# B's transposes moved between u and the first mix, its copies split over two engines, and four loads regrouped, in a fused adaptive-norm FFN kernel

## The reference

```
# layer 0
att   = softmax(mlp(cond))                            # (128, 8)
agg_w = einsum('bk,koi->boi', att, weight)            # a 32x32 mix for each sample
y     = einsum('boi,bih->boh', agg_w, x) + (att @ bias_k)[:, :, None]
gates = softmax(top2(y @ Wr.T))                       # 4 experts
x     = x + sum_e gates[e] * (y @ A[e].T) @ B[e].T * 4
# layer 1
o     = conv1d(x, convw, groups=4, 9 taps) + cond @ ctx_w.T + bias
w     = top-2 softmax weights of 8 experts, from relu(layernorm(o @ gw1.T + gb1)) @ gw2.T,
        zeroed for experts over a capacity that is counted over all tokens
x     = x + o @ weight.T + sum_e w[e] * (o @ lora_A[e]) @ lora_B[e] / 16
```

## Time and profile before

| | us |
|---|---|
| median of 3 runs | 302.68 |
| the three runs | 301.27, 302.68, 303.99 |
| the profiled execution | 302.07 |
| its span, first to last instruction | 300.3 |
| PE busy in it | 288.7 |

### The profile page before, as it was taken

One profiled execution on the slowest core, in us unless ns is written; L12 is line 12 of the kernel. 1 busy time (PEld: TensorE's weight loads), 2 busy tenths in 40 slices (PEclk: granted clock), 3 DMA queues, 4 the chain that ended last, 5 costly groups with the idle time before them and its releaser, 6 DMA issues.

```text
span 300.3 us, 6135 instructions
## 1 busy us (share of the span) xinstructions
PE 288.7 (96%) x1982; PEld 236.5 (79%) x1982; DVE 195.4 (65%) x506; ACT 125.3 (42%) x263; POOL 95.1 (32%) x124
## 2 busy tenths in 40 slices
PE   7999979999999999999999999999999999999994
PEld 5788957687978797879877987798777876777883
DVE  1655964743669466946594749474948555899885
ACT  3325834434622572258224822392237326103430
POOL 4361425123311431143114311431113235217660
PEclk9999999999999999999999999999999999999998
DMA  5796699893869487946794669458646790005887
GB/s 142 186 339 143 154 252 233 212 213 75 220 185 210 87 218 211 178 93 181 228 189 104 161 224 207 104 154 204 129 104 163 187 206 6 0 2 188 320 331 280
DMA packets 74400, 52.75 MB, mean 176 GB/s; under 512 B 44405, under 2 KB 61477, under 8 KB 74377
## 3 DMA queue, kind: packets, MB, share of 16 engines
q1 hardware_dynamic: 72936, 51.37, 69.1%
q10 hardware_dynamic: 1120, 1.07, 1.1%
q0 software_dynamic: 320, 0.02, 0.2%
HBM read 35.67 MB, written 16.78 MB: 175 GB/s over the span
## 4 chain that ended last, share of the span: by engine, by line
PE 54%; DMA 14%; SPq 12%; DVE 8%; issue 5%; ACT 4%; POOL 1%; DVEq 0%; ACTq 0%
PE ps_g L1139 10%; PE ps_d L1139 9%; DMA xg<-x1d 8%; PE ps_c L1277 7%; DMA x1d<-xq 7%; PE ps_a L1100 5%; PE ps_t L1293 3%; SPq L353 3%; PE ps_a L1089 3%; SPq L356 2%; ACT xq L632 2%; PE ps_d L1318 2%; PE ps_d L1319 2%; PE ps_d L1500 1%; PE ps_d L1505 1%
## 5 line engine op out<-in xcount | busy, mean ns | idle before, releaser
L512 POOL TENSOR_TENSOR o1l<-o,o1h 128x512 fp32r<-128x512 f32 x30 | 39.4, 1313 | 150.2 <-ACT o L644 150.2
L1139 PE MATMUL ps_d<-wt_hi,o1h 128*128 128x336 f32 (+1 forms) x120 | 41.1, 342 | 0.3 <-DVE y_all L961 0.3
L1139 PE MATMUL ps_d<-wt_hi,o1l 128*128 128x336 f32 (+1 forms) x120 | 38.7, 323 | 0.0
L1139 PE MATMUL ps_d<-wt_lo,o1h 128*128 128x336 f32 (+1 forms) x120 | 38.6, 322 | 0.0
L1277 PE MATMUL ps_c<-xg,cw 96*32 96x512 f32 x256 | 34.1, 604 | 3.1 <-DMA xg<-x1d 3.1
L955 DVE TENSOR_TENSOR oT<-ps_c,biasT 128x512 f32<-128x512 f32 x32 | 21.9, 686 | 22.8 <-PE ps_c L1277 21.9
L1139 PE MATMUL ps_g<-wt_hi,o1h 128*128 128x336 f32 x112 | 35.6, 318 | 0.6 <-ACT tmp_all L659 0.4
L1139 PE MATMUL ps_g<-wt_hi,o1l 128*128 128x336 f32 x112 | 35.5, 317 | 0.0
L1139 PE MATMUL ps_g<-wt_lo,o1h 128*128 128x336 f32 x112 | 35.4, 316 | 0.0
L632 ACT ACTIVATE xq<-y_all 128x512 f32 (+1 forms) x29 | 31.9, 1152 | 7.3 <-DMA x1d<-xq 4.1
L1100 PEld LDWEIGHTS ps_a<-pm,xT 128*128 128x128 f32 x256 | 30.2, 192 | 1.4 <-issue 0.8
(11 more groups left out here) (258 smaller groups left out, 577.7 us busy)
## 6 DMA issues: line engine op xcount, KB each, us to landing
xg<-x1d SPq DMA_DIRECT2D x64, 254.0 KB, 5.1
xg<-x1d SPq DMA_DIRECT2D x32, 256.0 KB, 3.8
x1d<-xq SPq DMA_DIRECT2D x30, 256.0 KB, 3.6
xs<-in_x_dram SPq DMA_DIRECT2D x6, 1024.0 KB, 6.2
out_dram<-xT SPq DMA_DIRECT2D x16, 256.0 KB, 2.1
out_dram<-xg SPq DMA_DIRECT2D x15, 256.0 KB, 2.1
y_all<-in_x_dram ACTq DMA_DIRECT2D x2, 512.0 KB, 5.2
y_all<-in_x_dram SPq DMA_DIRECT2D x1, 1024.0 KB, 5.7
```

The lines of the kernel that those rows point to most:

```text
L512: pool.tensor_tensor(lo, o1[t % 2][:, :, :], hi.bitcast(fp32), ALU.subtract).then_inc(s_o1l, 1)
L1139: last = T.matmul(bank[:, 0:columns], a[:, Q - 1 - q, :], w[:, q, first:first + columns], start=(q == 0 and n == 0), stop=(q == Q - 1 and ...
```

## The change

B's four transposes on PE move from between the first two tiles of `u_products(0)` to behind the last of them, where a fill stood. ScalarE copies the result twice, plain (`b_plain`, new) and rounded to `b_hi`; VectorE subtracts the two into `b_lo` behind `gates0(0)`, where before it made both parts from PSUM ahead of `mixbd`. `delta(0, 0)` waits for it. The transposes of `aw` move ahead of `attT`'s and VectorE's copy of them ahead of the context's; a second fill goes. The `aw` loads go ahead of the `mixw` loads. `bex`'s transpose and its copy to `biasT` move behind the first two transposes of step 1.

`ga` gets another layout, in blocks of 16 columns, so that one load with runs of 256 bytes brings all of `lora_a`, where eight with runs of 64 bytes did, and it is issued ahead of the taps. The x load of step 3 leaves the setup and is issued in SP's step 1, where the later steps have theirs.

```diff
@@ -29,6 +29,7 @@
...
     GC = G1 + ER1
+    GB = G1 // R1
     MC = (H + GC) // 2
@@ -63,6 +64,9 @@
...
             return v.broadcast_to(shape)
+
+        def blocks(v):
+            return v.rearrange("p q (e r) -> p e q r", r=R1)
@@ -92,7 +96,7 @@
...
         b_lo = sb("b_lo", [P, H], fp32r)
-        ga = sb("ga", [P, Q, GC])
+        ga = sb("ga", [P, GC // R1, Q, R1])
         cw = sb("cw", [P, G, Q, CG])
@@ -175,6 +179,7 @@
...
         pmsum = early(P, [UC])
+        b_plain = early(P, [HC, P])
@@ -200,7 +205,7 @@
...
         s_wk0 = sem("mix_zeros_ready")
-        names = ("condT", "pm", "h1", "ctxT", "b", "h2", "gw1", "att", "ctx", "rs", "attT", "wkr", "bias", "pmsum")
+        names = ("condT", "pm", "h1", "ctxT", "b", "h2", "gw1", "att", "ctx", "rs", "attT", "wkr", "bias", "pmsum", "b_hi", "b_plain")
         s_sp = {n: sem(f"setup_ps_{n}") for n in names}
@@ -331,13 +336,13 @@
...
             sp.dma_start(w2n, w2).then_inc(s_ld["w2"], 16)
+            sp.dma_start(aw[0:ER0], ffa.rearrange("e r h -> (e r) h")).then_inc(s_ld["aw"], 16)
+            sp.dma_start(aw[ER0:UC], ffr).then_inc(s_ld["aw"], 16)
             sp.wait_ge(s_wk0, 1)
...
                   .then_inc(s_ld["mixw"], 16)
-            sp.dma_start(aw[0:ER0], ffa.rearrange("e r h -> (e r) h")).then_inc(s_ld["aw"], 16)
-            sp.dma_start(aw[ER0:UC], ffr).then_inc(s_ld["aw"], 16)
             sp.dma_start(mbn, row(mixb, 1, BT)).then_inc(s_ld["mixb"], 16)
@@ -346,15 +351,13 @@
...
             sp.dma_start(gw2n, row(gw2, 1, NT)).then_inc(s_ld["gate"], 16)
-            for i in range(2):
-                sp.dma_start(xs[i][:, :, :], x_v[2 + i]).then_inc(s_x[i], 16)
+            sp.dma_start(xs[0][:, :, :], x_v[2]).then_inc(s_x[0], 16)
+            sp.dma_start(ga[:, GB:, :, :].rearrange("p e q r -> p e (q r)"),
+                         lora_a.rearrange("e (m q) r -> m e (q r)", q=Q)).then_inc(s_ld["lora_a"], 16)
             sp.wait_ge(s_zero, 1)
...
                              convw.rearrange("o c k -> c o k")).then_inc(s_ld["conv"], 16)
-            for e in range(E1):
-                sp.dma_start(ga[:, :, G1 + e * R1:G1 + (e + 1) * R1],
-                             lora_a[e].rearrange("(m q) r -> m q r", q=Q)).then_inc(s_ld["lora_a"], 16)
@@ -401,7 +404,7 @@
...
                         wait(sp, s_x1w[2], (s + 1) * 32)
-                if has(s, 2) and not at_step(s, 0) and not at_step(s, 1):
+                if has(s, 2) and not at_step(s, 0):
@@ -520,8 +523,8 @@
...
                     pool.wait_ge(s_gm, 2)
-                    pool.tensor_tensor(wt_lo[:, :, H:H + GC], ga[:, :, :], wt_hi[:, :, H:H + GC].bitcast(fp32),
-                                       ALU.subtract).then_inc(s_gal, 1)
+                    pool.tensor_tensor(blocks(wt_lo[:, :, H:H + GC]), ga[:, :, :, :],
+                                       blocks(wt_hi[:, :, H:H + GC].bitcast(fp32)), ALU.subtract).then_inc(s_gal, 1)
                     o1_low(0, 0)
@@ -599,8 +602,10 @@
...
             u_out(0)
-            act.wait_ge(s_sp["bias"], 1)
-            nc.scalar.activation(biasT[:, :], ps_t[:, 0:NB], ACT.Copy).then_inc(s_ss["bias"], 1)
+            act.wait_ge(s_sp["b"], 1)
+            nc.scalar.activation(b_plain.rearrange("p c m -> p (c m)"), ps_t[:, :], ACT.Copy).then_inc(s_ss["b_plain"], 1)
+            nc.scalar.activation(b_hi[:, :].rearrange("p (m c) -> p c m", c=HC),
+                                 ps_t[:, :].rearrange("p (c m) -> p c m", c=HC), ACT.Copy).then_inc(s_ss["b_hi"], 1)
@@ -608,6 +613,8 @@
...
             x_transposed(1, (0, 1))
+            act.wait_ge(s_sp["bias"], 1)
+            nc.scalar.activation(biasT[:, :], ps_t[:, 0:NB], ACT.Copy).then_inc(s_ss["bias"], 1)
             mix_copied(1, 2)
@@ -705,8 +712,8 @@
...
                     act.wait_ge(s_ss["gw1"], 1)
-                    act.wait_ge(s_ld["lora_a"], 16 * E1)
-                    nc.scalar.activation(wt_hi[:, :, H:H + GC], ga[:, :, :], ACT.Copy).then_inc(s_gah, 1)
+                    act.wait_ge(s_ld["lora_a"], 16)
+                    nc.scalar.activation(blocks(wt_hi[:, :, H:H + GC]), ga[:, :, :, :], ACT.Copy).then_inc(s_gah, 1)
                     gm_out(1)
@@ -833,6 +840,8 @@
...
             V.tensor_scalar(attw[:, :, 0:K0], row(atte, 1, 4), sm[:, 2:3], None, ALU.mult).then_inc(s_ss["att"], 1)
+            dve.wait_ge(s_sp["pm"], 1)
+            V.tensor_copy(pm[:, :, :].rearrange("p c u -> p (c u)"), ps_t[:, 0:HC * UC]).then_inc(s_ss["pm"], 1)
             dve.wait_ge(s_sp["ctx"], 1)
@@ -842,17 +851,9 @@
...
             V.tensor_copy(attT, ps_v[:, 0:P]).then_inc(s_ss["attT"], 1)
-            dve.wait_ge(s_sp["pm"], 1)
-            V.tensor_copy(pm[:, :, :].rearrange("p c u -> p (c u)"), ps_t[:, 0:HC * UC]).then_inc(s_ss["pm"], 1)
             dve.wait_ge(s_ss["pm"], 1)
...
-            dve.wait_ge(s_sp["b"], 1)
-            b_in = ps_t[:, :].rearrange("p (c m) -> p c m", c=HC)
-            link(V.tensor_copy(b_hi[:, :].rearrange("p (m c) -> p c m", c=HC), b_in))
-            V.tensor_tensor(b_lo[:, :].rearrange("p (m c) -> p c m", c=HC), b_in,
-                            b_hi[:, :].bitcast(fp32).rearrange("p (m c) -> p c m", c=HC),
-                            ALU.subtract).then_inc(s_ss["b"], 1)
             dve.wait_ge(s_mp0, 1)
@@ -863,6 +864,11 @@
...
             gates0(0)
+            dve.wait_ge(s_ss["b_hi"], 1)
+            dve.wait_ge(s_ss["b_plain"], 1)
+            V.tensor_tensor(b_lo[:, :].rearrange("p (m c) -> p c m", c=HC), b_plain,
+                            b_hi[:, :].bitcast(fp32).rearrange("p (m c) -> p c m", c=HC),
+                            ALU.subtract).then_inc(s_ss["b"], 1)
             dve.wait_ge(s_ld["rows"], 16 * 2)
@@ -970,7 +976,7 @@
...
                                       ps_v[G1 * t:G1 * t + G1, Q * G1:Q * G1 + E1])
-                    V.tensor_copy(ga[:, :, 0:G1], ps_v[:, 0:Q * G1].rearrange("p (q g) -> p q g", q=Q))\
+                    V.tensor_copy(ga[:, 0:GB, :, :], ps_v[:, 0:Q * G1].rearrange("p (q e r) -> p e q r", q=Q, r=R1))\
                      .then_inc(s_ss["gw1"], 1)
@@ -1186,25 +1192,20 @@
...
             t1(0, xs_early[0], 1)
-            keep_busy(1)
+            pe.wait_ge(s_ld["aw"], 32)
+            pe.wait_ge(s_attd, 1)
+            for c in range(HC):
+                last = T.transpose(ps_t[:, c * UC:(c + 1) * UC], aw[:, c * P:(c + 1) * P], ident[0:UC, 0:UC])
+            last.then_inc(s_sp["pm"], 1)
             pe.wait_ge(s_ss["att"], 1)
...
             t1(0, xs_early[0], 2)
-            pe.wait_ge(s_ld["aw"], 32)
-            for c in range(HC):
-                last = T.transpose(ps_t[:, c * UC:(c + 1) * UC], aw[:, c * P:(c + 1) * P], ident[0:UC, 0:UC])
-            last.then_inc(s_sp["pm"], 1)
             pe.wait_ge(s_xt, 2)
...
             pe.wait_ge(s_ss["pm"], 1)
-            u_products(0, (0,))
-            pe.wait_ge(s_bn, 1)
-            for c in range(HC):
-                last = T.transpose(ps_t[:, c * P:(c + 1) * P], bn2[:, c, :, :].rearrange("p d e -> p (d e)"), idp)
-            last.then_inc(s_sp["b"], 1)
-            u_products(0, (1,))
+            u_products(0, (0, 1))
             pe.wait_ge(s_attD, 1)
@@ -1218,13 +1219,14 @@
...
             u_products(0, (2, 3))
+            pe.wait_ge(s_bn, 1)
+            for c in range(HC):
+                last = T.transpose(ps_t[:, c * P:(c + 1) * P], bn2[:, c, :, :].rearrange("p d e -> p (d e)"), idp)
+            last.then_inc(s_sp["b"], 1)
             pe.wait_ge(s_bd, 1)
-            keep_busy(1)
             pe.wait_ge(s_mbsb, 1)
...
             mix(0)
-            pe.wait_ge(s_ss["b"], 1)
-            T.transpose(ps_t[:, 0:NB], bex, idp).then_inc(s_sp["bias"], 1)
@@ -1240,6 +1242,9 @@
...
             pe.wait_ge(s_ss["ctx"], 1)
+            pe.wait_ge(s_ss["b_hi"], 1)
+            pe.wait_ge(s_ss["b_plain"], 1)
+            T.transpose(ps_t[:, 0:NB], bex, idp).then_inc(s_sp["bias"], 1)
             mixture(1)
@@ -1304,7 +1309,7 @@
...
                         last = T.matmul(ps_g[:, 0:GC], o1[t % 2][:, Q - 1 - q, :],
-                                        ga[:, q, :], start=(q == 0), stop=(q == Q - 1))
+                                        ga[:, :, q, :], start=(q == 0), stop=(q == Q - 1))
                     last.then_inc(s_gp, 1)
@@ -1360,6 +1365,7 @@
...
                     pe.wait_ge(s_msa, 4)
+                    pe.wait_ge(s_ss["b"], 1)
                     delta(0, 0)
...
```

## The result

| | median, us | range | executions |
|---|---|---|---|
| before | 303.34 | 301.27 to 305.29 | 4 |
| the change | 307.62 | 304.87 to 308.39 | 4 |

The ratio is 1.019, 95% interval [1.013, 1.025]: some 2% slower, where 301.4 us and "about the same" were forecast. The profiled execution took 308.39 us, its span is 306.7, against 302.07 and 300.3. Such a ratio can mislead: the kernel before, timed once more against itself, came out at 1.0145 [1.0065, 1.0225] (experiment 4). What follows therefore rests on rows of the traces more than on this ratio.

The account below looks back on a forecast made before the run. TensorE, busy 288.7 of 300.3 us, bounds the kernel. -3.37 at conv(1,0) and +2.05 for the moved load give -1.3: span 299.0, 300.8 profiled, 301.4 on the median; range 299.2 to 303.5.

Parts of the forecast that it names:

- The load that is moved: SP's step 1: x3 ahead of gather(1,1) adds 2.8 us; PE stands 2.0, conv(1,1) starts at 63.05, gain 1.3.
- The price: x3's megabyte, added whole to gather(1,1)'s landing: 2.8 us taken, 2.4 by the landings' spacing, upper bound 4.2.
- The landing without x3: gather(1,1)'s landing before x3's price is added: 64.05 less 3.85 us, from an earlier gather(1,0).
- 378 GB/s: Mean DMA rate over the 2 us in which step 2 takes its x load; it priced 1.05 MB at 2.8 us.
- the 3.5: Upper sign before conv(1,1): the prediction is wrong if the idle there is under 1 or over 3.5 us.
- Rival 3: Clock falls in the setup or at the stand before conv(1,1); 4 us of matmuls at half speed give 305.4; chance 0.06.
- The setup: PE's work up to mix(0): earlier `aw` and moved transposes start mix(0) at 17.7 instead of 19.11, -1.4 us.
- nothing gained: Bound on `aw`'s landing in the setup: still 10.16, where 7.1 was taken from its 3.1 us earlier issue.
- SP's release: SP's queue free between 17 and 26.8 us, hidden because the first x1 tile is reordered only at 27.4.
- the gain at conv(0,0): No idle before conv(0,0), which starts near 36.6 us: -3.3.
- B's parts: ScalarE's copies (0.6 and 0.9 us) and VectorE's b_lo behind gates0(0) are free, 0.2 us to spare before delta(0,0).
- The rule: Transposes don't count as PE activity for the clock gate, so fewer fills and a 2 us stand would be riskier.

Follow-up runs that it names:

- experiment 4: Kernel before: one `lora_a` load 300.42 us; unchanged 305.38; four fills before conv(0,0) 301.68. The change with x3's load in the setup and eight `lora_a` loads: 304.94.
- experiment 3: Against the change: gather(1,2) issued only after gather(1,1) has landed, 307.03 us; x3's load issued behind gather(1,1) instead of ahead, 302.32 us.
- behind the taps: The change with x3's load back in the setup, issued behind the taps' loads: 301.21 us.
- the setup's order alone: The change with x3's load back in the setup and `lora_a` in eight loads behind the taps with the old `ga` layout: 304.94 us.
- the half behind: The change with x3's load in the setup and the second half of step 0's x on SP's queue behind `aw`: 299.57 us, ratio 0.995.

## Why the prediction was wrong

**The step that failed** is "The load that is moved": "I add the megabyte whole ... I take 2.8", "PE stands 2.0 us there". gather(1,1) landed at 67.06 in the profile (65.86 in the second), not at 63.0: the price of x3's load was taken too small, and the landing to which it was added too early.

*The price.* With x3 ahead, the gather's last part took 9.4 to 10.3 us from issue to landing (9.2 with (1,2) held back); without, 5.8 to 6.1 in four profiles. That is 3.3 to 4.5, and with the 0.5 that x3's own issue holds SP 3.8 to 5.0, where 2.8 were taken and 4.2 was the upper bound. 3.4 of it is the load's by experiment 3. That gather(1,2) takes part in the rest is possible, not shown; the prediction let it only "catch up".

*The landing without x3.* The step implies 60.2. Without x3 ahead of it the gather landed at 61.0 (behind the taps), 61.1 (x3 behind the gather) and 62.5 (in the setup). In the terms of the step, its last part was issued 2.66 later than implied (56.76 for 57.95 - 3.85 = 54.10), and from issue to landing went 10.30 instead of 6.1 + 2.8 = 8.9, so 1.40 more; together 4.06. Of the 2.66 some 2.0 stood before x3 was issued: gather(1,0) went at 51.73, not 3.85 ahead of its old 53.57.

*What the trace of before had.* The 378 GB/s are no price of the load by itself: in that trace the engines moved nearly as much from 58 to 60 us, when no x load was in flight. And its step 2 has the very order that the change makes in step 1, x's load right ahead of gather(2,1). SP in order of time, that part's source view, and the window:

```profile
86.53 0.86 SPq L376 DMA_DIRECT2D xg<-x1d  x1
```

```profile
DMA to landing us min/median/max: 8.1/8.1/8.1
```

```profile
58.00:60.00 2.00, 1.58 (x13) 0.54 (x11) 1.79 (x7) 0.00 (x0) 0.35 (x1) 1.00 1.08 355
```

8.1 us behind the load, with the engines all but empty (under 13 GB/s from 84 to 86) when it was issued; in the change they moved 216 to 290 when x3 was issued, and it took 10.3. The price had to be asked of the gather behind the load, and of what was in flight already. The stand, 3.6 to 4.8, passed the 3.5 that the prediction named as the point at which it would be wrong.

**The clock** was held up by the 1.97 us that "left the clock up" in one profile. That was one draw of two outcomes: the kernel before loses its clock in about four executions of ten (39 of 92), in the one that was profiled behind 2.23 us of idle. Rival 3 (slower, 305.4, given 0.06) named the mechanism and one of its places, and was priced too low by the stand: of the 6.4 us lost in the profile 2.9 are the clock's, the rest is waiting, net of the early gain. From 67 to 73 us the clock stood at 0.50, six us in which about three us' worth of work was done. The prediction read a single execution's clock row as a property of the kernel.

**The setup**: -1.4 at mix(0) was -0.19. `aw`, issued at 3.1, landed at 10.1 as before; "nothing gained" was named as a bound, and was true. Behind it sat a second step that the prediction passed over: the transposes of x's third and fourth tile are now queued behind `pm`'s on PE, so the xT copies that u_products waits for came at 11.16 instead of 10.01 + 0.60. With `aw` on time the gain was 0.5, so even the better landing is not worth 1.4. Whether the MLP's chain, 0.6 to 0.8 us later (ScalarE's exponential at 8.97 and 8.82 in the change's two profiles and 9.06 with the half behind, for 8.21), is also the loads' doing was not tried.

**Right were**: SP's release by 25.7 (within 17 to 26.8) and its being hidden, the first write as soon as its tile was there (28.70; forecast 27.5, late by the setup's 1.2), no idle before conv(0,0), 0.30 before gm_transposed(1) (forecast 0.35), the gain at conv(0,0) but for the setup's share (37.74; 36.6) and so at conv(0,1) (43.08; 41.9) and conv(1,0) (56.99; 55.71). B's parts were free: ScalarE, and VectorE's low part behind the gates, in order of time:

```profile
18.70 0.60 ACT L606 ACTIVATE y_all<-ps_t 128x512 f32<-128x512 f32 x1
19.20 1.09 ACT L607 ACTIVATE b_hi<-ps_t 128x512 fp32r<-128x512 f32 x1
```

```profile
24.26 1.11 DVE L869 TENSOR_TENSOR b_lo<-y_all,b_hi 128x512 fp32r<-128x512 f32 x1
```

delta(0,0) waited for neither. The high part took 1.09, not 0.9.

**The sum**: forecast 299.0 of span. conv(1,1) at 67.10 instead of 63.05 adds 4.05 (conv(1,0) was 1.28 late already). The clock adds 2.9 and the later waits 0.75: 306.7.

**The rule** that the prediction weighed, from the Trainium skill's "TensorE: Matmul & The Clock Gate", section "Part 4: PE-mode transpose": the fall behind 1.2 us of idle and a run of transposes fits it, but the same transposes behind 0.43 us, in the profile of the change, and behind 1.11 us, with the setup's order alone, left 1.00. One case in 18 does not settle it.

**Open** stays why the lower of before's two times goes down to 299.6: its profile of 302.07 has the clock up and a span of 300.3, and no faster execution was profiled. And no kernel took the transposes alone, so the share of idle and of transposes in the setup's fall isn't separated.

## What to carry to other kernels

Ask of a moved load not how many bytes it has but who is queued behind it at its new place and how much slack that one has; put ahead of a gather with 0.3 to 1.3 us to spare, a megabyte held its landing up by some 4 to 5 us, and most of that became a stand; one place further back it held the next gather up by as much, and the stand was under 1. An idle of 2 us on PE costs 2 us once and some 3 more whenever the clock falls with it (1.5 to 2.9 in the change's two profiles), so look at several executions' mean clock before calling a stand harmless, and try a fill in a stand that can't be removed. Regrouping many small loads into one (`lora_a`) was enough for the early gain here; the load moved beside it would have been too, but gave back more than all of it.

## What was not expected of the hardware

- The granted clock fell behind idle of 2.22, 2.23, 2.77, 3.49, 3.56 and 4.77 us, and once behind 1.20 followed by transposes; it stayed up behind 1.97, 1.11 and 0.43. It was then at 0.50 for 3 to 17 us of work. Twice it fell only after PE had work again: behind the 2.23 at 42 to 43 us, with matmuls from 40.37 on, and behind the 3.56 at 67 to 68, with matmuls from 65.90 on.
- The load of a row of 8 KB, issued at 3.74 on SP's queue, landed after 6.33 us while 0.5 MB on ScalarE's queue were in flight; with that half issued behind it, nobody waited for it.
- The DMA engines show a full share (1.23) at 213 GB/s in the change from 64 to 66 us, and 1.08 at 355 GB/s in the kernel before from 58 to 60: a share of the engines says nothing of bytes.
